# Linear attention, score matmuls: the two heads of a pair issued in alternation instead of one after the other

## What is computed

```python
keys    = _l2norm(x @ Wk); queries = _l2norm(x @ Wq); values = x @ Wv      # per head
beta    = sigmoid(x @ Wbeta)
decay   = exp(minimum(cum_log[t] - cum_log[s], 0)) * triu                   # s >= t
kq      = einsum('bhtd,bhsd->bhts', queries, keys) / sqrt(64)
out     = einsum('bhts,bhsd->bhtd', kq * decay, values) + beta * values
return out @ Wout
```

## Time and profile before

| | |
|---|---|
| median of 3 runs | 4999.79 us (4998.96 to 5003.04) |
| the profiled execution | 4999.74 us |
| its span, first to last instruction | 4998.0 us |
| outside the span | 1.7 us |
| mean granted TensorE clock | 0.900 of full speed |
| PE busy | 4497.6 us (90%) |
| DVE, ACT, POOL busy | 48%, 35%, 17% |
| L1045, all 64 pairs | 109.4 us with at least one in flight |

### The profile page before, as it was taken

How to read it: one execution, slowest core, us unless ns; L and a number is a source line. 1 busy time by engine, 2 the same in 40 slices (tenths; PEclk the granted TensorE clock), 3 DMA queues, 4 the chain that set the end, 5 groups by cost and what they waited for, 6 DMA issues and landing times.

```text
span 4998.0 us, 76578 instructions
## 1 busy us (share of the span) xinstructions
PE 4497.6 (90%) x30219; PEld 2825.7 (57%) x30275; DVE 2393.4 (48%) x6906; ACT 1724.4 (35%) x3496; POOL 842.3 (17%) x1313
## 2 busy tenths in 40 slices
PE   7988989889898898988989889898898998988989
PEld 4556545565455654557545575455754557545575
DVE  3435544355443654435544355444554445544455
ACT  2333433234332343323433234333343333433334
POOL 2003110030110301113011140111401114011140
PEclk8999979999799998999989999899998998988989
DMA  2000000000000000000000000000000000000000
GB/s 67 1 1 1 1 6 1 1 1 1 6 1 1 1 1 6 1 1 1 1 6 1 1 2 1 6 1 1 2 1 6 1 1 2 1 3 1 1 1 3
DMA packets 19571, 17.25 MB, mean 3 GB/s; under 512 B 2462, under 2 KB 18799, under 8 KB 19183
## 3 DMA queue, kind: packets, MB, share of 16 engines
q1 hardware_dynamic: 19183, 11.99, 0.8%
HBM read 9.89 MB, written 2.10 MB: 2 GB/s over the span
## 4 chain that ended last, share of the span: by engine, by line
PE 79%; POOL 7%; DVE 6%; ACT 5%; issue 3%; DVEq 0%; ACTq 0%; POOLq 0%; SPq 0%
PE banks L982 7%; PE banks L986 7%; PE banks L885 7%; PE banks L972 7%; PE banks L913 6%; PE banks L830 6%; POOL work L483 4%; PE banks L924 3%; PE banks L870 3%; PE banks L1178 3%; PE banks L1165 2%; PE banks L1199 2%; PE banks L1072 2%; PE banks L1045 2%; PE banks L1021 2%
## 5 line engine op out<-in xcount | busy, mean ns | idle before, releaser
L1367 DVE CUSTOM_DVE_ANT_0 work<-banks,mask_row 128x512 f32<-128x512 f32 (+3 forms) x1024 | 452.3, 489 | 260.7 <-PE banks L885 254.5
L885 PE MATMUL banks<-work 32*128 32x128 f32 (+3 forms) x2048 | 534.0, 550 | 24.6 <-DVE work L1367 24.6
L437 POOL TENSOR_TENSOR rstd<-rstd,half 128x1 f32<-128x1 f32 x256 | 134.2, 550 | 2470.6 <-DVE moments L1295 1899.7
L913 PE MATMUL banks<-work 32*128 32x256 f32 (+3 forms) x2048 | 527.6, 522 | 11.0 <-ACT work L643 9.1
L643 ACT ACTIVATE work<-banks 128x384 f32<-128x384 f32 (+1 forms) x768 | 374.6, 529 | 461.0 <-PE banks L913 455.2
L659 ACT ACTIVATE work<-banks 128x512 f32<-128x512 f32 (+1 forms) x384 | 228.9, 596 | 698.6 <-PE banks L982 698.4
L1439 DVE TENSOR_TENSOR work<-work,banks 128x512 f32<-128x512 f32 (+1 forms) x384 | 263.6, 686 | 355.5 <-PE banks L986 355.2
L982 PE MATMUL banks<-xnT,wg 128*128 128x512 f32 (+1 forms) x768 | 423.6, 635 | 0.0
L986 PE MATMUL banks<-xnT,wu 128*128 128x512 f32 (+1 forms) x768 | 412.0, 619 | 0.0
L972 PEld LDWEIGHTS banks<-wd,work 128*128 128x128 f32 (+1 forms) x3072 | 360.6, 191 | 57.3 <-issue 57.3
L885 PEld LDWEIGHTS banks<-work 32*128 32x128 f32 x2048 | 292.3, 222 | 166.9 <-DVE work L1367 110.4
(11 more groups left out here) (255 smaller groups left out, 7252.4 us busy)
## 6 DMA issues: line engine op xcount, KB each, us to landing
x_next<-in_L_attn_a_x_dram SPq DMA_DIRECT2D x8, 256.0 KB, 2.8
out_dram<-x SPq DMA_DIRECT2D x8, 256.0 KB, 2.2
wg<-in_L_ffn_Wg_dram SPq DMA_DIRECT2D x1, 1376.0 KB
wu<-in_L_ffn_Wu_dram SPq DMA_DIRECT2D x1, 1376.0 KB
wd<-in_L_ffn_Wd_dram SPq DMA_DIRECT2D x2, 512.0 KB
wk_l<-in_L_attn_a_Wk_dram SPq DMA_DIRECT2D x1, 512.0 KB, 7.2
wv_l<-in_L_attn_a_Wv_dram SPq DMA_DIRECT2D x1, 512.0 KB, 6.7
wq_l<-in_L_attn_a_Wq_dram SPq DMA_DIRECT2D x1, 512.0 KB, 6.8
```

The lines of the kernel that those rows point to most:

```text
L885: m = eng.matmul(bank(k % 3)[:, col:col + N], q4[own, G, P * t:P * t + P], k4[own, G, 0:N], start=True, stop=True)
L913: m = eng.matmul(bank(3 + c % 3)[:, col:col + N], k4[own, G, P * s:P * s + P], q4[own, G, P * s:T], start=True, stop=True)
L1367: m = eng.tensor_tensor_reduce(out=summed[:, k % 2, col:col + N], in0=bank(k % 3)[:, col:col + N], in1=mask_row[:, T - N:T], scale=1.0, sc ...
```

## The change

The loops over the head and over the row block change places, so that consecutive matmuls of a pair lie in different halves of the array's rows and in different banks. Before, head 0 of pair `c` waited for the mask of head 0 of the pair before, and head 1 for that of head 1. Now both wait once, ahead of the first matmul, for both masks (`l_wts` at `2c`). The two increments of `l_sc` are on each head's last matmul, as before; they now come one after the other at the end.

```diff
             def scores(c):
-                for r in range(2):
-                    h = 2 * c + r
-                    if h >= 2:
-                        eng.wait_ge(l_wts, h - 1)
-                    else:
-                        eng.wait_ge(l_qk, 2 * NC2)
-                    for t in range(NT):
+                if c >= 1:
+                    eng.wait_ge(l_wts, 2 * c)
+                else:
+                    eng.wait_ge(l_qk, 2 * NC2)
+                for t in range(NT):
+                    for r in range(2):
                         m = eng.matmul(bank(r)[:, P * t:P * t + P], l_kT[64 * r:64 * r + 64, c, P * t:P * t + P],
                                        l_qT[64 * r:64 * r + 64, c, P * t:P * t + P], start=True, stop=True)
-                    m.then_inc(l_sc, 1)
+                        if t == NT - 1:
+                            m.then_inc(l_sc, 1)
```

## The result

The changed kernel takes 4971.62 us (median of six runs, 4970.35 to 4989.29) against 5000.23 us for the kernel before: a ratio of 0.9947, 95% interval 0.9931 to 0.9963. It is faster by 0.53%; 4973 was forecast. The profiled execution took 4971.78 us.

The account below looks back on a forecast made before the run. PE, busy 90% of the span, was taken as the bound. 2.7 us ahead of the outputs plus 2.3 gave 5.0; less 1.7, 3.3 us per turn; eight turns, 26.4, taken from 4999.74 gave 4973 us; range 4960 to 5001.

Parts of the forecast that it names:

- The overlap: Score matmuls of a pair: both heads side by side take 1.09 us instead of 1.64, saving 0.55 us per pair.
- The drain rival: Score matmuls: each change of array half drains the array, 2.4 us per pair, 5049 us; chance 0.06, shared with slower clock patterns.
- The loop: All pairs ahead of the last outputs: 0.3 + 1.1 + 1.36 = 2.7 us saved per turn.
- pairs 0 and 1 together: First two pairs: pair 0 saves nothing, the common wait costs 0.04 us, pair 1 gains about 0.3 us.
- pairs 2 and 3: Middle pairs, nothing waits near PE: the full 0.55 us each, 1.1 us in all.
- pairs 4 to 7: Last four pairs: only 0.34 of the 0.55 us gained in each, 1.36 us in all.
- the forecast gap of 0.21 us: PE ahead of the outputs in pairs 4 to 7: the rest of the 0.55 us becomes a 0.21 us stall.
- the 1.93 us: PE's wait for pair 7's summed states ahead of the last outputs, expected to stay at 1.93 us.
- The clock in the layer: Last outputs to projection: outputs at full clock save another 2.3 us, projection 5.0 us earlier, net 3.3 us per turn.
- Loss on the projection: Projection: a cold stretch of 3.42 us (clock at half) lies over it and costs 1.7 us per turn.
- the case in which the turns take it back: Whole turn: cold stretches level the saving out, turns stay 621.2 us apart, 4999.8 us; chance 0.13.
- a deciding point of 1.9 us: Ahead of the last outputs: the clock takes the saving back if under about 1.9 us is left there.

Follow-up runs that it names:

- The run in twos: Changed kernel with matmuls alternating two by two: blocks 0 and 1 of each head, then blocks 2 and 3 of each; 4987.18 us, ratio 0.9971.
- the run with the wait alone: Kernel before, heads still one after the other, with only the common wait for both masks added; 4999.74 us, ratio 0.9998.
- the state copies first on the kernel before: Kernel before, heads one after the other, with ScalarE's column copies moved one pair later; 4985.14 us, ratio 0.9963.
- the kernel with the state copies first: Changed kernel with ScalarE's column copies moved one pair later; 4955.59 us, ratio 0.9912, and 4955.25 us, ratio 0.9906, in a second set of runs.

## Why the prediction was right, and where it was lucky

**The overlap.** 1.09 us per pair was forecast from head 1's own run in the old order, and 1.09 came. The drain rival is dead: seven changes of half per pair, 1.09 us; three, 1.19. The rule of strict program order (the Trainium skill, TensorE: Matmul & The Clock Gate, "What overlaps and what doesn't") would have made the saving 0.9 us per pair. The trace disagrees: 0.55. The run in twos disagrees too, with a matmul of the second half that starts ahead of three issued before it.

**The loop.** Forecast in front of the last outputs: 2.7 us. Measured from each turn's first scores: 41.07 before, 38.29 after, 2.78. Its terms: pairs 0 and 1 together 0.32 (the first outputs begin 4.83 and 4.51 us after the first scores; forecast 0.3); pairs 2 and 3 1.10 (forecast 1.1); pairs 4 to 7 1.35 (forecast 1.36). In those four rounds the chain holds the first four output matmuls for 0.60 us instead of 0.39: the forecast gap of 0.21 us, ended by L1503. That ScalarE's order makes this gap and the 1.93 us is shown by the experiment that moves it.

**The clock in the layer.** Last outputs at full clock: forecast 2.40 us, measured 2.48. Projection 5.0 us earlier: measured 5.07. Loss on the projection 1.7: measured 9.04 - 7.41 = 1.63. The layer ends 3.44 us earlier per turn (forecast 3.3). Up to here the forecast was right in its mechanism and in every term.

**From the layer to the turn.** This step was weak, and the forecast's good number owes something to chance. I carried 3.3 us per turn to the end unchanged, and gave the case in which the turns take it back its own chance, with a deciding point of 1.9 us. The runs show neither a proportional law nor that point: 1.3 us saved ahead of the outputs gave a whole step, 2.6 us mostly none. My argument against this case, that the clock falls after idle time of PE, fits the layer and not the whole turn: in the run in twos the clock fell at 1333.75 with PE busy without a gap since at least 1316.9. Every turn in the twelve profiled executions of eleven kernels is 614.4, 617.8, 621.2, 624.6 or 628.1 us long, 3.41 apart; only two turns, the first ones behind late prologues, lie elsewhere (618.9 and 618.7). One turn of the run with the wait alone was 624.6 too. Work saved or added in the layer chooses a step: 0.7 us saved ahead of the last outputs gave no step, 1.3 us a whole one, 2.2 us (the state copies first on the kernel before) and 2.6 us (the alternation in twos) a step in two of seven turns each, 2.8 us a whole step in all; 1.8 us added cost one or two steps. The changed kernel's 3.44 us happened to be the size of one step. Why the alternation in twos ended between the two others is shown only as far as its place: a cold stretch more in an attention 317 us later. What decides whether it comes is not shown.

**The spread of the runs.** After, 4970.35 to 4989.29 us. The range of several steps of 3.41 us fits turns that fall on another step in some executions. That this happens is shown for the kernel with the state copies first, the one kernel with two profiled executions: they have two and six turns of 617.8 us, and their first scores are at 401.77 and 390.15, so the work ahead of the first turn varies too. Of the changed kernel one execution was profiled, so for its own spread this is argued and not shown.

## What to carry to other kernels

Matmuls that use different halves of the array's rows overlap only as far as the issue order brings them near each other: alternate them one by one. Look in the old trace for places where two such groups already meet, they give the price. Then follow what the shorter step meets next, in each round of the loop, since of 8 x 0.55 = 4.4 us per turn only 2.8 passed the masks of pair 0 and a chain on ScalarE and VectorE. And where the clock rises and falls in a loop, don't read a change of under one per cent as so many microseconds of work: compare the lengths of the turns, and the cold stretches in layers that were not touched.

## What the runs showed of the hardware

- Matmuls over the upper and the lower 64 rows of the array, in f32 with 128 columns, run side by side: 16 in 1.09 us, where one half after the other took 1.64, with 0.11 us from matmul to matmul in each half.
- The turns' lengths stand on steps 3.41 us apart, over eleven kernels whose linear attention differs by up to 10 us in length (48.8 to 58.7 from the first scores to the end of the projection).
- The granted clock fell to half with PE busy without a gap, on matmuls over 32 of the 128 rows (1331.80 to 1336.5 in the run in twos, the fall at 1333.75); in another turn of the same execution the same work ran at full clock (1955.00 to 1961.70).
